# Delta-rule attention between two ternary FFNs: the state update as four f16 products, the keys' diagonal blocks placed by SyncE's DMAs, and new ticks

## The reference, cut to what matters

```
x = x + 0.5 * ffn(layernorm(x))
x = x + attn(layernorm(x))            # attn has its own norm, bias and residual
x = x + 0.5 * ffn(layernorm(x))

ffn: h = silu(w1 x) * (w2 x); h = gelu(h1 h); h = gelu(h2 h); w3 h     # ternary weights, 1024 hidden
attn, 16 heads of 16: q, k, v, beta = split(normed @ w_qkvb + b); beta = sigmoid(beta); k = k / |k|
  for t in 0..1023:                   # S is 16 x 16 per batch and head
    S = S + beta_t * (v_t - S k_t) (x) k_t
    o_t = S q_t
  out = x + o @ w_out + b_out
```

## Time and profile before

| | value |
|---|---|
| median of three runs | 1703.59 us (1702.45 to 1703.64) |
| the profiled execution's own time | 1703.29 us |
| its span | 1701.5 us |
| busy PE, DVE, ACT, POOL | 97%, 74%, 74%, 75% |
| granted TensorE clock, mean | 0.998 |
| two costliest lines of PE | L1152 (h1, h2, w3), L1135 (w1, w2) |

### The profile page before, as it was taken

The page is one execution under the profiler, slowest core; times in us unless marked ns, Lnnn a source line. Parts: engine busy times, 40 slices in busy tenths (PEclk is TensorE's granted clock), DMA queues, the critical chain, the costliest instruction groups (busy, mean ns, idle before and its releaser), DMA issues.

```text
span 1701.5 us, 31307 instructions
## 1 busy us (share of the span) xinstructions
PE 1651.6 (97%) x10385; PEld 1016.2 (60%) x10385; DVE 1258.3 (74%) x3152; ACT 1251.0 (74%) x2510; POOL 1279.5 (75%) x1594
## 2 busy tenths in 40 slices
PE   6989999999999999999999999999999999999999
PEld 5765556565656555565656565555656565655578
DVE  5456787878788787878787887878787878878541
ACT  4668687777778686887777786867877777867654
POOL 4574887969686877869696868778696868687563
PEclk9999999999999999999999999999999999999999
DMA  7200000000000000000000000000000000000000
GB/s 279 75 1 1 1 2 1 2 1 1 1 26 1 1 1 1 26 1 2 1 26 1 2 1 1 1 1 26 1 1 1 2 1 14 1 3 12 13 2 13
DMA packets 5279, 23.26 MB, mean 14 GB/s; under 512 B 640, under 2 KB 1664, under 8 KB 3584
## 3 DMA queue, kind: packets, MB, share of 16 engines
q1 hardware_dynamic: 5120, 21.26, 3.4%
HBM read 17.06 MB, written 4.19 MB: 12 GB/s over the span
## 4 chain that ended last, share of the span: by engine, by line
PE 60%; DVE 12%; POOL 8%; ACT 6%; issue 5%; DVEq 0%; POOLq 0%; ACTq 0%
PE ffn_bank L1152 37%; PE att_bank L1173 6%; PE ffn_bank L1135 5%; PE state_bank L1211 3%; POOL hid_lo L600 3%; POOL pairs L629 2%; DVE terms L998 2%; PE att_bank L1188 2%; PE att_bank L1189 2%; PE att_bank L1220 2%; ACT state_parts L783 2%; PE att_bank L1103 2%; DVE state_bank L1000 2%; DVE roots L875 1%; POOL pairs_lo L637 1%
## 5 line engine op out<-in xcount | busy, mean ns | idle before, releaser
L1152 PE MATMUL ffn_bank<-hid_hi,w_sb 128*128 128x448 f16 (+1 forms) x2880 | 941.0, 337 | 7.6 <-ACT hid L732 3.8
L1152 PE MATMUL ffn_bank<-hid_lo,w_sb 128*128 128x448 f16 (+1 forms) x2880 | 940.9, 337 | 0.0
L600 POOL TENSOR_TENSOR hid_lo<-hid,hid_hi 128x448 f16<-128x448 f32 (+1 forms) x480 | 466.2, 989 | 180.8 <-ACT hid_hi L708 180.6
L1152 PEld LDWEIGHTS ffn_bank<-hid_hi,w_sb 128*128 128x128 fp8e4 x2880 | 285.6, 99 | 210.6 <-issue 10.8
L1152 PEld LDWEIGHTS ffn_bank<-hid_lo,w_sb 128*128 128x128 fp8e4 x2880 | 282.1, 98 | 209.2 <-issue 14.7
L629 POOL TENSOR_TENSOR pairs<-KQ 128x288 f32<-128x288 f32 (+15 forms) x496 | 319.9, 667 | 108.2 <-DVE KQ L925 105.5
L637 POOL TENSOR_TENSOR pairs_lo<-pairs,pairs_hi 128x448 f16<-128x448 f32 (+15 forms) x416 | 319.7, 784 | 31.5 <-ACT pairs_hi L797 31.5
L708 ACT CAST hid_hi<-hid 128x448 f16<-128x448 f32 (+1 forms) x480 | 240.1, 537 | 35.7 <-DVE hid L897 32.9
L732 ACT ACTIVATE hid<-ffn_bank,par_sb 128x448 f32<-128x448 f32 (+1 forms) x320 | 175.6, 600 | 110.9 <-PE ffn_bank L1152 103.9
L797 ACT CAST pairs_hi<-pairs 128x448 f16<-128x448 f32 (+15 forms) x416 | 168.6, 439 | 81.4 <-POOL pairs L629 76.2
L1135 PE MATMUL ffn_bank<-xn_hi,w_sb 128*128 128x448 f16 (+1 forms) x640 | 211.7, 340 | 16.2 <-DVE hid L897 9.0
(11 more groups left out here) (95 smaller groups left out, 2220.7 us busy)
## 6 DMA issues: line engine op xcount, KB each, us to landing
NK<-in_w SPq DMA_DIRECT2D x11, 1024.0 KB, 5.9
X<-in_x SPq DMA_DIRECT2D x7, 512.0 KB, 3.7
out<-X SPq DMA_DIRECT2D x7, 512.0 KB, 2.6
wqkvb_sb<-in_wqkvb SPq DMA_DIRECT2D x1, 1024.0 KB, 8.5
X<-in_x SPq DMA_DIRECT2D x2, 256.0 KB, 6.5
out<-X SPq DMA_DIRECT2D x2, 256.0 KB, 2.1
wout_sb<-in_wout SPq DMA_DIRECT2D x1, 256.0 KB, 9.6
par_sb<-in_par SPq DMA_DIRECT2D x1, 24.0 KB, 2.5
```

What stands on the lines that cost most here:

```text
L600: pool.tensor_tensor(hid_lo[layer % 2][:, m, 0:call.width], hid[:, u % HID_BUFFERS, 0:call.width], hid_hi[layer % 2][:, m, 0:call.width], ...
L1152: mm = nc.tensor.matmul(ffn_ps(call, j), weight(name, kk, 2 * pair + i), v[:, kk, cols], start=kk == 0 and part == 0, stop=kk == KT_FF - 1 ...
```

## The change

The state update's operands become f16, each as a high and a low part, and the update becomes four products per group pair: both parts of Kz by both parts of U. The keys' parts exist already (KQ_parts); DVE now transposes both parts at once, into an f16 KTr with a part dimension. U is split newly: `high_u` on ACT casts it (three ticks ahead of the update), `low_u` on POOL subtracts (in the same tick's place), and `turn_u` moves from one tick to five ahead. Kz's diagonal blocks are written by four SyncE DMAs per chunk in place of four ACT copies, and the store and the refill of X get places among them, at ticks 3 and 10. The semaphore kz_ready counts 16 per DMA. All tick tables, leads and lags change.

```diff
-E_RETR = [2, 22, 43, 66]
-E_STATE = [16, 37, 58, 83]
-E_PROJ = {K_: 41, Q_: 46, V_: 46, B_: 41}
-E_NORM = 42
-E_OUT = 49
-E_QK = [0, 3, 7, 5, 21, 10, 21, 16, 22, 28, 31, 27, 31, 38, 39, 41]
+E_RETR = [1, 22, 45, 67]
+E_STATE = [17, 39, 58, 81]
+E_PROJ = {K_: 40, Q_: 54, V_: 52, B_: 40}
+E_NORM = 44
+E_OUT = 57
+E_QK = [1, 11, 5, 14, 3, 7, 11, 29, 21, 22, 36, 32, 30, 43, 40, 54]
-E_KK = dict(zip(KK_ROWS, [57, 60, 60, 64, 64, 70, 74, 77, 75, 80, 84, 86, 87, 89, 84]))
-PAIR_LEAD = {"whole": 1, "half": 22}
-HIGH_LEAD, LOW_LEAD = 9, 6
-ACT_LAG, POOL_LAG, DVE_LAG = 2, 5, 1
-SPLIT_LAG, SPREAD_LAG = 1, 4
-E_KQ_HIGH, E_K_LOW, E_Q_LOW = 59, 74, 71
-E_O_LOW = 80
+E_KK = dict(zip(KK_ROWS, [56, 57, 63, 64, 66, 66, 66, 73, 75, 84, 82, 86, 83, 87, 60]))
+PAIR_LEAD = {"whole": 12, "half": 11}
+HIGH_LEAD, LOW_LEAD = 7, 3
+ACT_LAG, POOL_LAG, DVE_LAG = 1, 4, 1
+SPLIT_LAG, SPREAD_LAG = 2, 4
+E_KQ_HIGH, E_K_LOW, E_Q_LOW = 67, 68, 77
+E_O_LOW = 72
+TURN_LEAD, U_HIGH_LEAD, U_LOW_LEAD = 5, 3, 3
+E_STORE, E_REFILL = 3, 10
-    ffn_ln: sum=at, mean=at + 4, center=at + 4, square=at + 4, sq_sum=at + 3, var=at + 9, root=at + 10, recip0=at + 10, recip1=at + 11, recip2=at + 11, recip3=at + 13, norm=at + 17, apply=at + 26, low=at + 24
+    ffn_ln: sum=at + 2, mean=at + 5, center=at + 4, square=at + 7, sq_sum=at + 7, var=at + 11, root=at + 10, recip0=at + 14, recip1=at + 15, recip2=at + 17, recip3=at + 19, norm=at + 19, apply=at + 21, low=at + 20
-LN_ATT = dict(sum=14, mean=12, center=21, square=22, sq_sum=22, var=31, root=33, recip=33, norm=37, y_recip=41, apply=36, low=37)
-LN_FFN = 52
-SAVE_LAG = 3
+LN_ATT = dict(sum=11, mean=15, center=18, square=17, sq_sum=26, var=26, root=25, recip=30, norm=39, y_recip=39, apply=40, low=44)
+LN_FFN = 64
+SAVE_LAG = 1
...
-        KTr = sb("KTr", [P, 2, GP, 32])
-        Kz = sb("Kz", [P, GP, P])
+        KTr = sb("KTr", [P, 2, 2, GP, 32], F16)
+        Kz = sb("Kz", [P, 2, GP, P], F16)
+        Uz_parts = sb("Uz_parts", [P, 2, GP, 64], F16)
...
+            def make_kz(w, c):                       # SyncE; on ACT before, with act.copy
+                i = w * HCH + c
+                if i:
+                    sp.wait_ge(dstate_ready, i)
+                sp.wait_ge(k_turned, i + 1)
+                for q in range(QUADS):
+                    rows = slice(q * 32, (q + 1) * 32)
+                    sp.dma_start(Kz[rows, :, :, q * 32:(q + 1) * 32], KTr[rows, c % 2, :, :, :]).then_inc(kz_ready, 16)
+            for f in FRAMES:
+                for e in range(TICKS):
+                    for s in range(SLABS - 1):
+                        if f == call_of(2, s, HALVES - 1).n - 1 and e == E_STORE:
+                            store(s)
+                        if f == call_of(2, s, HALVES - 1).n - 1 and e == E_REFILL and s + RING < SLABS:
+                            refill(s)
+                    for c in range(HCH):
+                        if 0 <= f < PARTS and e == E_RETR[c] + 1:
+                            make_kz(f, c)
...
+            def low_u(w, c):                         # POOL
+                i = w * HCH + c
+                pool.wait_ge(u_hi_ready, i + 1)
+                pool.tensor_tensor(Uz_parts[:, 1, :, :], Uz[:, :, :, :].rearrange("p g b w -> p g (b w)"), Uz_parts[:, 0, :, :], ALU.subtract).then_inc(u_ready, 1)
...
+            def high_u(w, c):                        # ACT
+                i = w * HCH + c
+                if i:
+                    act.wait_ge(dstate_ready, i)
+                act.wait_ge(u_turned, i + 1)
+                act.copy(Uz_parts[:, 0, :, :], Uz[:, :, :, :].rearrange("p g b w -> p g (b w)")).then_inc(u_hi_ready, 1)
...
-                    dve.wait_ge(k_ready, 2 * w + 2)
+                    dve.wait_ge(kq_ready, 2 * w + 1)
-                nc.vector.transpose(KTr[:, c % 2, :, :].rearrange("p g w -> p (g w)"), KQ[:, 0, chunk * GB * C:(chunk + 1) * GB * C]).then_inc(k_turned, 1)
+                nc.vector.transpose(KTr[:, c % 2, :, :, :].rearrange("p a g w -> p (a g w)"),
+                                    KQ_parts[:, :, 0, chunk * GB * C:(chunk + 1) * GB * C]).then_inc(k_turned, 1)
...
-                        if e == E_STATE[c] - 1:
+                        if e == E_STATE[c] - TURN_LEAD:
                             turn_u(f, c)
...
                 for g in range(GP):
-                    mm = nc.tensor.matmul(state_ps[:, g * 64:(g + 1) * 64], Kz[:, g, :], Uz[:, g, :, :].rearrange("p b w -> p (b w)"),
-                                          start=False, stop=True, skip_group_check=True)
+                    for k_part in range(2):
+                        for u_part in range(2):
+                            mm = nc.tensor.matmul(state_ps[:, g * 64:(g + 1) * 64], Kz[:, k_part, g, :], Uz_parts[:, u_part, g, :],
+                                                  start=False, stop=True, skip_group_check=True)
```

More of the change, by code:

```diff
@@ L169 @@
 QUARTERS = 4
+TURN_LEAD, U_HIGH_LEAD, U_LOW_LEAD = 5, 3, 3
 def ffn_ln(at):
-    return dict(sum=at, mean=at + 4, center=at + 4, square=at + 4, sq_sum=at + 3, var=at + 9, root=at + 10, recip0=at + 10, recip1=at + 11, recip2=at + 11, recip3=at + 13, norm=at + 17, apply=at + 26, low=at + 24)
+    return dict(sum=at + 2, mean=at + 5, center=at + 4, square=at + 7, sq_sum=at + 7, var=at + 11, root=at + 10, recip0=at + 14, recip1=at + 15, recip2=at + 17, recip3=at + 19, norm=at + 19, apply=at + 21, low=at + 20)
 def half_ln(at):
     return dict(sum=at + 5, mean=at + 2, center=at + 3, square=at + 8, sq_sum=at + 5, var=at + 7, root=at + 9, recip0=at + 9, recip1=at + 9, recip2=at + 11, recip3=at + 12, norm=at + 13, apply=at + 13, low=at + 14)
-LN_ATT = dict(sum=14, mean=12, center=21, square=22, sq_sum=22, var=31, root=33, recip=33, norm=37, y_recip=41, apply=36, low=37)
-LN_SECOND = dict(sum=20, mean=34, square=37, sq_sum=27, var=39, root=48, apply=60, low=69)
-LN_FFN = 52
+LN_ATT = dict(sum=11, mean=15, center=18, square=17, sq_sum=26, var=26, root=25, recip=30, norm=39, y_recip=39, apply=40, low=44)
+LN_SECOND = dict(sum=25, mean=22, square=29, sq_sum=31, var=43, root=42, apply=58, low=63)
+LN_FFN = 64
 JOBS = []
@@ L555, in _ @@
             pool.memset(state_parts[:, :, :, :], 0.0).then_inc(state_ready, 1)
-            pool.memset(Kz[:, :, :], 0.0).then_inc(kz_zeroed, 1)
+            pool.memset(Kz[:, :, :, :], 0.0).then_inc(kz_zeroed, 1)
             pool.wait_ge(side_ready, 4)
@@ L647, in add_o_low @@
                 pool.tensor_tensor(O[:, mine], O[:, mine], O_low[:, :], ALU.add).then_inc(o_low_added, 1)
+            def low_u(w, c):
+                i = w * HCH + c
+                pool.wait_ge(u_hi_ready, i + 1)
+                pool.tensor_tensor(Uz_parts[:, 1, :, :], Uz[:, :, :, :].rearrange("p g b w -> p g (b w)"), Uz_parts[:, 0, :, :], ALU.subtract).then_inc(u_ready, 1)
             def attention(f, e):
+                if 0 <= f < PARTS:
+                    for c in range(HCH):
+                        if e == E_STATE[c] - U_LOW_LEAD:
+                            low_u(f, c)
                 if f + 1 < PARTS and e == E_K_LOW:
@@ L757, in key_root @@
                 act.activation(k_sq[:, :], bank_of("norm", w, 0)[:, :], ACT.Sqrt).then_inc(att_read_s, 1)
-            def make_kz(w, c):
-                i = w * HCH + c
-                if i:
-                    act.wait_ge(dstate_ready, i)
-                act.wait_ge(k_turned, i + 1)
-                for q in range(QUADS):
-                    rows = slice(q * 32, (q + 1) * 32)
-                    act.copy(Kz[rows, :, q * 32:(q + 1) * 32], KTr[rows, c % 2, :, :]).then_inc(kz_ready, 1)
             def save_q(w, c):
@@ L1004, in turn_u @@
                 dve.wait_ge(solve_step, (i + 1) * STEPS * 2)
-                nc.vector.transpose(Uz[:, :, :, :], gapped()).then_inc(u_ready, 1)
+                nc.vector.transpose(Uz[:, :, :, :], gapped()).then_inc(u_turned, 1)
             def split_state(w, c):
```

19 lines of the change are left out of this document (10 added, 9 removed).

## The result

The changed kernel takes 1685.8 us (median of 4, 1685.35 to 1686.65) against 1703.0 us (median of 4, 1702.45 to 1703.64) of the kernel before on the same chip: ratio 0.9899, 95% interval 0.9882 to 0.9917. It is faster by 17.2 us, where the forecast had 34.3.

What follows compares the result with a forecast made beforehand. PE, busy 97% of the span, was taken as the bound, so shorter slots save time. 1703.3 - 28.8 - 8 - 3 + 5 + 2 was given as 1669 us (the terms make 1670.5); own range 1658 to 1677, 8-in-10 range 1652 to 1692.

Steps and rivals of the forecast that it cites:

- The slot: State update's slot on PE: sixteen f16 products take 0.46 us in place of 0.91, over 64 updates 28.8 us off.
- Waits ahead of the update: PE's idle time before updates, 10 us over 16 frames, goes with turn_u five ticks ahead: 8 us off.
- ACT's relief: ACT loses 256 Kz copies (75 us) and gains 26 us of casts; PE's early-frame waits shrink, 3 us off.
- DVE's transpose at nothing: Keys' transpose on DVE grows by under 28 us in all, ahead of DVE's wait for the retrieval: costed at nothing.
- SyncE at nothing: Four Kz DMAs per chunk take 4.3 us against windows of 13 us or more: costed at nothing.
- the bound of 15.9: Kz lands late, a rival: 4.3 + 11.6 us against 13, PE waiting in two chunks a frame, 1762 us; chance 0.03.
- The third chunk: Rival: POOL comes late to the third chunk's low_u, PE stands 3.3 us more in each of 16 frames, 1722; chance 0.07.
- (a): Feed-forward norm's last steps at later ticks: 4 us added once in frame -1 (bounds 0 and 8), 1 us in the last frame.
- The feared wait for xn_lo: In frame -1 PE wants xn_lo at tick 88, 16 us after the sum, for a chain that had 36 ticks; 4 us added.
- 1 us likewise: Last frame: 1 us added for the later feed-forward norm, as in frame -1.
- (b): Query and value projections and output at later ticks: 2 us added for small new waits, bounds -6 and +24.
- the wide range: Range of the kernel's time given for 8 times in 10: 1652 to 1692 us.

## Why the prediction was right or wrong

**The slot (28.8 off): right.** 0.46 us in 64 updates, 28.2 by the frames' own reading. That needs one remark: in the kernel with the new ticks the f32 slot is 0.84, so against what stays possible in f32 the products save 24 us. How much of that reaches the time is another matter: 8.8 us. The rule of the Trainium skill, "TensorE: Matmul & The Clock Gate", section "Back-to-back issue gap", some 81 ns per pair of weight load and matmul at 128 columns, doesn't describe this stream of 64 columns: 0.46/16 = 29 ns per pair, in the update as in the retrieval.

**Waits ahead of the update (8 off): failed.** This is the step on which the steady frame turned. The forecast counted the chain by its durations (1.5 us against 5 of lead) and took POOL's queue as a bound only. The old waits did go: with turn_u five ticks ahead and the f32 form no update waits, 0.8 us a frame or 13 us, more than the 8 counted. But with the hop the four updates wait 0.41 + 0.17 = 0.58 us a frame, 9.3 us, so that under 4 of the 8 us are left; and 0.42 more stands ahead of two retrievals that had none to speak of, 0.23 of it only with the f16 form. Without low_u the update waits vanish and the time falls by 10.5 us, so the price of that hop is shown. The wait at tick 39 has two parts: low_u stands behind two hid_lo, and it takes 1.12 us in place of 0.67. The earlier low_u removes both, and then the norm's chain is the one that ends last.

**ACT's relief (3 off): failed.** In the new order ACT's copies are not on the path: with 102.7 us of them on ACT the time is the same. (With the ticks of before this wasn't tried.) Slots 9 and 11 wait 1.4 us a frame now, 1.0 before, and 1.3 with the f32 form and the new ticks. They are DVE's: reordering DVE changes them, in both directions, loading ACT again doesn't lengthen them. How much of the 0.84 us in slot 11 belongs to the query rows is 0.34; the rest of both slots wasn't separated.

**DVE's transpose at nothing: not refuted.** 0.43 us for 256 f16 columns, 27.8 us in all, against 0.30 and 19.2 before: 8.6 us more of DVE's time, where the forecast allowed under 28. No run isolates it. The retrieval's wait of 0.19 us at tick 45 is there with the f32 transpose too and isn't its doing; the 0.23 at tick 22 comes with the f16 form and stays without low_u, so it could hold a part, which is open.

**SyncE at nothing: right.** One DMA lands 1.9 us after its issue, and the four of a chunk take 3.8 us (5.0 at most) from the first issue to the last landing: the forecast had 4.3, and the bound of 15.9 is far. The last landing is 7.0 us or more ahead of its update in all 64 chunks. q1's packets went from 5120 to 74752, and its share of 16 engines' span from 3.4 to 5.7%.

**The third chunk (rival, slower): didn't happen.** The update of tick 58 has no wait in a steady frame of the kernel after. With the old ticks it waits 2.5 us in a steady frame and 1.7 or more in each, so the margin was the right place to look at, and the new ticks keep it.

**The new ticks, (a) (4 on in frame -1, 1 in the last): wrong in sign and in size.** Frame -1 takes 2.7 us less, and the stretch before it 2.5, of which a part is chance. The kernel before waits 2.1 and 2.4 us at ticks 54 and 56 of frame -1 and runs at a granted clock of 0.95 there; after, no wait in that frame is over 1.7 us and the clock is 1.00. The waits over 0.3 us hardly differ in sum (8.2 and 7.5 us), so most of the 2.7 us is the clock:

```profile
60.70:121.90 61.20, 54.83 (x427) 43.95 (x425) 30.44 (x52) 42.35 (x86) 43.05 (x58) 1.00 0.00 1
```

The feared wait for xn_lo is there, but only 1.1 us. In the last frame the "1 us likewise" was 8.9, which is the second step that failed. I gave it a figure by analogy and didn't walk the queues of ACT and POOL behind that norm. Moving it by six ticks alone gives back 5.6 us, and spreading it another 1.5, which is within the noise: this is the mis-sized term. What is left of frame 16 are the query pairs (1.1 and 1.6 us for POOL's pairs_lo at ticks 29 and 36) and 1.1 us for O at tick 57; none was tried.

**(b) (2 on for small waits): low.** The projections and the output show no new wait over 0.1 us in a steady frame. What is new stands elsewhere: ahead of two retrievals (0.42) and of the frame's first product (0.18), 0.6 us a frame or some 10 us, against 2 counted. Half of it (0.20 at tick 45, 0.10 at the first product) and the 0.25 more in slot 11 are there with the f32 form too, so these are the ticks'; the rest is the f16 form's.

In sum the mechanism was right where it counts the slot, and wrong in taking the chain behind it as free: on an f32 kernel with the new ticks the products bring 8.8 us and not 24. The other 8.4 come with the ticks, which the forecast had at a cost of 7, with 8 and 3 off for the waits and for ACT. The total came to half the forecast because errors of both signs met, so that 1685.8 lies in the wide range is in part luck. By its terms the forecast had 32.8 us, and the spans give 18.0. Of the 14.8 between, 15.2 are frames 0 to 15 (waits were to fall by 9 us net and rose by some 5), 7.9 the last frame and 0.9 head and tail, while 9.2 came back ahead of frame 0.
